# A message-passing layer on one core: the edge loop in pairs of tiles, with semaphores and one-hot buffers per target tile

## The reference, cut to what matters

```
msgs = x[src]; s = segment_sum(msgs, dst); c = segment_sum(1, dst)
agg  = s / maximum(c, 1)
x    = x + (agg @ W_l.T + x_norm @ W_r.T + b_r)     # x_norm: the rows of x, normalised
... layer norm and RMS norm of the new rows, attention over the 625 rows with rotary embedding
```

## Time and profile before

| what | value |
|---|---|
| median of three runs | 1066.08 us |
| profiled execution, its span | 1070.24 us, 1068.4 us |
| PE busy | 967.0 us (91%) |
| DVE, ACT, POOL busy | 466.6, 278.7, 130.2 us |
| edge matmuls (line 568) | 480 records, 55.0 us busy |
| granted PE clock over the span | 0.942 |

### The profile page before, as it was taken

One profiled execution on the slowest core, in us unless ns is written; L12 is line 12 of the kernel. 1 busy time (PEld: TensorE's weight loads), 2 busy tenths in 40 slices (PEclk: granted clock), 3 DMA queues, 4 the chain that ended last, 5 costly groups with the idle time before them and its releaser, 6 DMA issues.

```text
span 1068.4 us, 15246 instructions
## 1 busy us (share of the span) xinstructions
PE 967.0 (91%) x5585; PEld 782.8 (73%) x5585; DVE 466.6 (44%) x1426; ACT 278.7 (26%) x624; POOL 130.2 (12%) x135
## 2 busy tenths in 40 slices
PE   5999899889999999889998989999999998899896
PEld 5988454789999867688976768777786554566785
DVE  6658634542222330452259997522435143332222
ACT  3110034212222012313336764232111111124010
POOL 3010000023231110024410000000101000000241
PEclk9899778999999989999988999899899999899998
DMA  9100000138897512229542000053200000231762
GB/s 330 67 0 1 1 1 0 49 114 331 308 334 279 187 65 80 69 86 306 175 143 83 1 2 1 30 195 139 79 1 1 1 1 1 118 118 53 245 227 73
DMA packets 26278, 114.71 MB, mean 107 GB/s; under 512 B 5096, under 2 KB 9102, under 8 KB 19050
## 3 DMA queue, kind: packets, MB, share of 16 engines
q1 hardware_dynamic: 20647, 97.09, 25.5%
q0 software_dynamic: 5568, 16.78, 4.8%
HBM read 102.05 MB, written 11.81 MB: 107 GB/s over the span
## 4 chain that ended last, share of the span: by engine, by line
PE 71%; DVE 13%; DMA 6%; issue 5%; ACT 3%; POOL 1%; SPq 1%; DVEq 0%; POOLq 0%; ACTq 0%
PE PS L726 7%; PE PS L415 6%; PE PS L568 5%; PE PS L784 4%; PE PS L741 4%; PE PS L1110 4%; PE PS L770 3%; PE PS L392 3%; PE PS L426 3%; PE PS L484 3%; DMA arena<-flat_rows,route 3%; PE PS L806 2%; DVE arena L1806 2%; PE PS L610 2%; PE PS L854 2%
## 5 line engine op out<-in xcount | busy, mean ns | idle before, releaser
L392 PE MATMUL PS<-const 128*128 128x128 f32 x780 | 103.9, 296 | 7.8 <-DVE X L1177 2.1
L392 PEld LDWEIGHTS PS<-const 128*128 128x128 f32 x780 | 99.4, 209 | 12.9 <-issue 4.2
L726 PEld LDWEIGHTS PS<-HT,ring 128*128 128x128 f32 x680 | 78.4, 192 | 3.4 <-issue 2.6
L726 PE MATMUL PS<-HT,ring 128*128 128x128 f32 x680 | 78.8, 275 | 2.2 <-DVE HT L1701 1.3
L2417 POOL DMA_INDIRECT slot_rows<-ST,route x46 | 46.4, 1009 | 169.1 <-ACT ST L2167 99.7
L2365 POOL TENSOR_TENSOR col<-col,power 125x5 f32<-125x5 f32 x8 | 9.4, 1177 | 454.9 <-DVE col L1192 344.8
L1698 DVE TENSOR_TENSOR HT<-HT,PS 128x256 f32<-128x256 f32 (+1 forms) x51 | 19.2, 376 | 93.6 <-ACT HT L2156 73.7
L568 PE MATMUL PS<-HT 125*125 125x250 bf16 x480 | 55.0, 277 | 3.4 <-DVE HT L1574 3.4
L568 PEld LDWEIGHTS PS<-HT 125*125 125x125 bf16 x480 | 53.5, 141 | 3.8 <-DVE HT L1574 3.8
L928 PE MATMUL PS<-arena,HT 125*33 125x125 f32 x400 | 53.7, 283 | 0.0
L741 PE MATMUL PS<-ring,HT 128*128 128x256 f32 x204 | 46.7, 379 | 0.0
(11 more groups left out here) (430 smaller groups left out, 1736.0 us busy)
## 6 DMA issues: line engine op xcount, KB each, us to landing
ring<-in_experts SPq DMA_DIRECT2D x17, 1386.0 KB
ring<-in_experts SPq DMA_DIRECT2D x17, 768.0 KB, 5.8
ring<-in_experts SPq DMA_DIRECT2D x11, 1026.0 KB
arena<-in_experts SPq DMA_DIRECT2D x6, 1026.0 KB
ring<-in_experts SPq DMA_DIRECT2D x6, 1024.0 KB, 7.9
arena<-in_experts SPq DMA_DIRECT2D x6, 1024.0 KB
arena<-in_gnn SPq DMA_DIRECT2D x5, 1024.0 KB, 5.8
ring<-in_experts SPq DMA_DIRECT2D x8, 513.0 KB, 3.7
```

What stands on the lines that cost most here:

```text
L392: pe.matmul(PS[:, bank, 0:128], ident, ident, start=True, stop=True)
L726: mm = pe.matmul(PS[:, bank, at:at + SLOTS], both[:, j, k, m * 128:(m + 1) * 128], xs[0][i % 2][:, k, :], start=(k == 0), stop=(k == KD - 1))
```

## The change

- `GE` is 2: the runs are found in pairs of edge tiles. Each d always does the two tiles of its first pair outside the loop, and the loop does four tiles a turn. From the same targets this gives 18, 22, 18, 18 and 18 edge tiles, 94 in all.
- Each d has its own `onehots` and `edge_mm` semaphore, and even and odd d have one-hot buffers of their own, four tiles each. `shifts` and the third register load are gone: PE loads one register for each d (`further`), DVE two (one for d = 0).
- The count comes from two matmuls of 200 columns in place of one of 400, and DVE's reduction of line 1505 is gone; the 24 filler matmuls behind the count become 20. ACT makes the casts of the two number patterns, which DVE made.
- Two W_r products and the sum of tile 0 move from behind d = 2 to behind d = 1; the sum of tile 1 is alone behind d = 2 with three W_r products; behind d = 3 and d = 4 PE's work is as before. On DVE `both_types` and `finish` come ahead of the register loads of the next d, and the tiles 1 and 2 are finished later or one step apart.
- POOL's addition of the bias row waits for the sixth ACT copy, that is, until after the loop of d = 1.
- The causal mask is filled ahead of the last `finish`; POOL takes the two powers in two instructions of five columns; XN is written behind the copies of the transposes (`residual_norm`).

```diff
-GE = 4
+GE = 2
...
-        onehots, edge_mm = sem("onehots"), sem("edge_mm")
+        onehots, edge_mm = ([sem(f"{x}{d}") for d in range(NT)] for x in ("onehots", "edge_mm"))
...
+        src_hot = [HT[0:TP, r * hot_size:r * hot_size + 4 * 313].bitcast(BF16).rearrange("p (q n) -> p q n", q=4)
+                   for r in range(2)]
+        dst_hot = [HT[0:TP, r * hot_size + 4 * 313:(r + 1) * hot_size].bitcast(BF16).rearrange("p (q n) -> p q n", q=4)
+                   for r in range(2)]
...
-                mm = pe.matmul(PS[0:1, 7, 0:NT * ET], above[:, 0, 0:1], inside_flat, start=True, stop=True)
+                pairs = inside_flat.rearrange("p (g q) -> p g q", q=GE)
+                for q in range(GE):
+                    mm = pe.matmul(PS[0:1, 7, 0:NT * NG], above[:, 0, 0:1], pairs[:, :, q], start=(q == 0), stop=(q == GE - 1))
...
-                for _ in range(24):
+                for _ in range(20):
...
-                    if d == 2:
-                        for t in range(NT):
-                            root_tile(side_bank(), XT, wr_, t * TP, TP).then_inc(act_full, 1)
-                    for t in {2: (0, 1), 3: (2,), 4: (3,)}.get(d, ()):
-                        sum_tile(t, side_bank()).then_inc(act_full, 1)
+                    for t in {1: (0, 1), 2: (2, 3, 4)}.get(d, ()):
+                        root_tile(side_bank(), XT, wr_, t * TP, TP).then_inc(act_full, 1)
+                    if d:
+                        sum_tile(d - 1, side_bank()).then_inc(act_full, 1)
...
-                def limits(d):
-
-                    if d == 1:
-                        pe.wait_ge(ranges_ready, 2)
-                    start = pe.value_load(ranges[0:1, d:d + 1], min_val=0, max_val=NG - 1)
-                    stop = pe.value_load(ranges[0:1, NT + d:NT + d + 1], min_val=1, max_val=NG)
-                    return start, stop, pe.value_load(ranges[0:1, 2 * NT + d:2 * NT + d + 1], min_val=0, max_val=NT * NG)
+                def further(d):
+
+                    return pe.value_load(ranges[0:1, d:d + 1], min_val=0, max_val=NG - 1)
...
-                    with pe.Fori(start, stop) as i:
-                        for q in range(GE):
-                            pe.wait_ge(onehots, shift * GE + i * GE + (q + 1))
-                            for m in range(NT):
-                                mm = pe.matmul(PS[0:TP, base + m // 2, m % 2 * 2 * TP:(m % 2 + 1) * 2 * TP],
-                                               src_hot[:, q, m * TP:(m + 1) * TP], dst_hot[:, q, :],
-                                               start=False, stop=False)
-                            mm.then_inc(edge_mm, 1)
+                    for q in range(2):
+                        pe.wait_ge(onehots[d], q + 1)
+                        edge_tile(q)
+                    with pe.Fori(0, more, 2) as i:
+                        for q in range(4):
+                            pe.wait_ge(onehots[d], 2 * i + (q + 3))
+                            edge_tile((q + 2) % 4)
...
+            def residual_norm():
+
+                mv = col[:, 64:64 + NT * 2].rearrange("p (t s) -> p t s", t=NT)
+                dve.wait_ge(rms_ready, 1)
                 for t in range(NT):
                     ins = dve.tensor_scalar(XN[:, t, :], X[:, t, :], mv[:, t, 0:1], col[:, 8 + t:9 + t],
                                             ALU.subtract, ALU.mult)
...
-                dve.wait_ge(patterns_out, 2)
-                dve.tensor_copy(iota16, numbers[:, 0:626]).then_inc(patterns_ready, 1)
-                dve.tensor_copy(target16.rearrange("p d c -> p (d c)"), numbers[:, 626:626 + 2 * NT * TP]
-                                ).then_inc(patterns_ready, 1)
...
-                dve.tensor_reduce(found, PS[0:1, 7, 0:NT * ET].rearrange("p (d g q) -> p d g q", d=NT, q=GE), AX.X,
-                                  ALU.add).then_inc(dve_free, 7)
-                dve.wait_ge(dve_free, 7)
...
-                def shifts():
-
-                    link(dve.tensor_tensor(lim[:, 3, :], lim[:, 1, :], lim[:, 0, :], ALU.subtract))
-                    link(dve.memset(lim[:, 2, :], float(NG)))
-                    for d in range(1, NT):
-                        link(dve.tensor_tensor(lim[:, 2, d:d + 1], lim[:, 2, d - 1:d], lim[:, 3, d - 1:d], ALU.add))
-                    link(dve.tensor_tensor(lim[:, 2, :], lim[:, 2, :], lim[:, 0, :], ALU.subtract))
-                    dve.tensor_copy(ranges[:, 2 * NT + 1:3 * NT], lim[:, 2, 1:NT]).then_inc(ranges_ready, 1)
+                def further(d):
+
+                    first = dve.value_load(ranges[0:1, NT + d:NT + d + 1], min_val=0, max_val=NG) if d else 0
+                    return first, dve.value_load(ranges[0:1, d:d + 1], min_val=0, max_val=NG - 1)
...
-                    dve.wait_ge(act_free, 15 + t)
+                    dve.wait_ge(act_free, (12, 16, 17, 18)[t])
...
-                    with dve.Fori(start, stop) as i:
-                        for q in range(GE):
-                            j = bass.ds(i * GE + q, 1)
-                            dve.wait_ge(edge_mm, shift * GE + i * GE + (q + 1))
-                            dve.tensor_scalar(src_hot[:, q, :], iota16, srcf[:, j], None, ALU.is_equal)
-                            dve.tensor_scalar(dst_hot[:, q, :], target16[:, d, :], keyf[:, j], None,
-                                              ALU.is_equal).then_inc(onehots, 1)
-                    if d == 0:
-                        shifts()
-                    if d + 1 < NT:
-                        start, stop, shift = limits(d + 1)
+
+                    def edge_tile(q, j):
+
+                        dve.tensor_scalar(src_hot[d % 2][:, q, :], iota16, srcf[:, j], None, ALU.is_equal)
+                        dve.tensor_scalar(dst_hot[d % 2][:, q, :], target16[:, d, :], keyf[:, j], None,
+                                          ALU.is_equal).then_inc(onehots[d], 1)
+
+                    for q in range(2):
+                        edge_tile(q, bass.ds(first * 2 + q, 1))
+                    with dve.Fori(0, more, 2) as i:
+                        for q in range(4):
+                            dve.wait_ge(edge_mm[d], 2 * i + (q + 3))
+                            edge_tile((q + 2) % 4, bass.ds((first + i) * 2 + (q + 2), 1))
                     if d:
                         both_types(d - 1)
-                    for t in {3: (0,), 4: (1, 2)}.get(d, ()):
-                        finish_taken(t)
+                    if d in (2, 3):
+                        finish_taken(d - 2)
+                    if d + 1 < NT:
+                        first, more = further(d + 1)
...
+                finish_taken(NT - 3)
                 finish_taken(NT - 2)
+                dve.memset(ahead_mask[:, 0:N - TP], 0.0)
+                dve.wait_ge(tables_in, 32)
+                dve.tensor_copy(ahead_mask[:, N - TP:N], CONST(const, "causal", TP))
...
                 layer_and_rms_norm()
                 take_transposes(XT, scale=COLS(cols, "ln1_w"))
+                residual_norm()
...
+                act.wait_ge(patterns_out, 1)
+                act.activation(iota16, numbers[:, 0:626], ACT.Copy).then_inc(patterns_ready, 1)
+                act.wait_ge(patterns_out, 2)
+                act.activation(target16.rearrange("p d c -> p (d c)"), numbers[:, 626:626 + 2 * NT * TP], ACT.Copy
+                               ).then_inc(patterns_ready, 1)
...
             pool.wait_ge(xn_ready, NT)
+            pool.wait_ge(act_free, 6)
             pool.tensor_tensor(X[:, :, :], X[:, :, :], ROWS(rows, "l0_b_r", TP).unsqueeze(1).broadcast_to([TP, NT, D]),
                                ALU.add).then_inc(root_added, 1)
             pool.wait_ge(root_added, 1)
             for t in range(NT):
-                pool.wait_ge(act_free, 10 + t)
+                pool.wait_ge(act_free, 10 + t + (t > 1))
                 pool.tensor_tensor(X[:, t, :], X[:, t, :], ROOT[:, t, :], ALU.add).then_inc(root_added, 1)
             pool.wait_ge(var_ready, 2)
-            two = col[:, 0:208].rearrange("p (a n) -> p a n", a=2)
-            pool.tensor_tensor(two[:, :, 8:8 + NT], two[:, :, 0:NT], power[:, :].unsqueeze(1).broadcast_to([TP, 2, NT]),
-                               ALU.pow).then_inc(rstd_ready, 1)
+            pool.tensor_tensor(col[:, 112:112 + NT], col[:, 104:104 + NT], power[:, :], ALU.pow).then_inc(rstd_ready, 1)
+            pool.tensor_tensor(col[:, 8:8 + NT], col[:, 0:NT], power[:, :], ALU.pow).then_inc(rms_ready, 1)
```

82 lines of the change are left out of this document (41 added, 41 removed).

## The result

| | before | after |
|---|---|---|
| median, first chip | 1068.19 us (1058.96 to 1071.42, 4 runs) | 1049.11 us (1044.76 to 1053.44, 4 runs) |
| median, second chip | 1066.04 us (1060.91 to 1069.42, 11 runs) | 1047.56 us (1043.15 to 1050.09, 6 runs) |
| profiled execution, its span | 1070.24, 1068.4 us | 1044.76, 1042.8 us |
| granted PE clock over the span | 0.942 | 0.958 |
| first score matmul of the attention | 127.83 us | 111.29 us |

The ratio is 0.9841 [0.9802, 0.9880] on the first chip and 0.9814 [0.9787, 0.9841] on the second: 17 and 20 us less (the brackets hold a 95% interval; the difference of the first chip's medians, taken by itself, is 19 us). The forecast was 1052 us, in 1044 to 1062.

A forecast was written before the change was run, and what follows sets the result against it. PE was taken as the bound, through its gaps and slow clock in the first 125 us. Terms summed to 12.15 us, 17.65 with the clock: 1053.9 or 1048.4 from the 1066.08 median, 1052.6 from the profile; forecast 1052, range 1044 to 1062.

The forecast's parts named there:

- Term 1: Start, ahead of the first edge matmul: fewer register loads and an earlier edge key save 2.1 us (ends 1.3 and 2.5).
- Term 2: Loop of d = 0: moving POOL's bias row addition beside PE's W products saves 2.2 us (ends 2.2 and 0).
- Term 3: Ahead of PE's transposes: without the shifts most of the 2.25 us wait goes, saving 1.5 us (ends 1.0 and 2.0).
- Term 4: Edge loops: 94 tiles for 96, at 0.545 us a tile, save 1.1 us.
- The rival that DVE becomes the pace: Edge loops: DVE's tile time over 0.545 us costs 0.9 us per 0.01 over 94 tiles; at 0.65, 1062 us; chance 0.04.
- Terms 5 to 7: PE's waits between loops shrink: loads at d = 1 and 2 save 1.0 us, d = 3 0.65, d = 4 1.2.
- Term 8: Loop of d = 1: with both long gaps ahead gone, the clock recovers, saving 2.5 us, transposes included (ends 0 and 2.7).
- Term 9: Norm behind the last sum: earlier mask, five-column powers and XT copies not behind XN save 2.4 us (end 1.4).
- Term 10: Projection to rotary part: with shorter gaps PE runs at 2.4 GHz, 11.5 us for 14.5, saving 3.0 (ends 0 and 3.0).
- the stall moved: First rival: POOL's additions meet DVE's tiles for d = 2 or d = 3, giving 1056 us; chance 0.12.
- the clock fell again: Rival: transposes alone or half-microsecond gaps bring the clock down, leaving a gain of 8 to 10 us, 1057; chance 0.12.
- the attention did not get slower: Rival, slower: attention starts in another phase and half of a possible clock loss gives 1078 us; chance 0.06.

The follow-up runs named there:

- Three loads: The changed kernel with three register loads for each target tile on both engines, as before, the further values unused; 1050.43 us (1 run).
- Casts on DVE: The changed kernel with the two pattern casts back on DVE, ahead of the copy of dst; 1043.42 us (1 run).
- shifts back: The changed kernel with the chain of the shifts back on DVE behind the loop of d = 0, results unused; 1046.79 us (4 runs), ratio 0.9828.
- bias row early: The changed kernel with POOL's addition of the bias row early again, waiting only for the normalised rows; 1043.38 us (1 run).
- XT first: Two versions of the changed kernel: ACT copies the transposes ahead of the adjacency, 1045.86 us (6 runs); the same with six filler matmuls added, 1043.79 us (6 runs).
- loads first: The changed kernel with DVE's register loads ahead of `both_types` and the finish, and one finish moved; 1049.20 us (1 run).
- norm order back: The changed kernel with the mask, the power of ten columns and XN where before has them; 1047.46 us (4 runs), ratio 0.9829.
- side work back: The changed kernel with W_r products and sums where before has them, and tile 1's finish behind the last addition of types; 1038.12 us (1 run).

## Why the prediction was right

The forecast, 1052 us, is 3 us above the first chip's median and 4 above the second's. It was right by its terms of order, which the runs bear out; that the sum came so near is in part luck, as the terms show. From the two profiles, each term with what it measured:

- **Term 1, start, 2.1 forecast:** 2.0, of which 0.33 is the key (done at 8.17, forecast 8.1) and 1.68 the gap. Three loads gives the loads 1.24 of the gap. The other 0.44 (2.64 before, 2.20 there) goes with the two tiles outside the loop; no run has that alone. Casts on DVE shows no more than 0.2.
- **Term 2, POOL's stand, 2.2:** 2.2, shown from both sides.
- **Term 3, shifts, 1.5:** the 2.25 us wait is gone and 0.2 of it came back as a longer way through the transposes, so 2.0. Up to 0.6 of this is clock: the transposes took 2.37 us in before and 1.73 in after, waits left out. By order it is 1.4. The size is near, but the chain alone was not the cause: the wait was the chain and three loads in a row (shifts back), and with one load left the chain costs nothing.
- **Term 4, tiles, 1.1:** 1.3. The five loops at full clock are 4 x 9.84 + 11.98 = 51.3 us against 8.98 + 13.05 + 8.77 + 2 x 10.91 = 52.6 before. The rival that DVE becomes the pace is out: a tile takes 0.547 us.
- **Terms 5 to 7, between loops, 1.0 + 0.65 + 1.2:** 1.5 + 0.9 + 1.2. I took a third of each wait to stay with one load of three; nothing stayed. One load leaves no idle time on PE at all.
- **Term 8, clock in the loop of d = 1, 2.5:** 0.7. This step failed. With the transposes, which it included at 0.3, it is at most 1.3. Both long gaps are gone, and after's profile still has 0.60 from 22 to 26 us. Before's loop in its own timeline:

```profile
28.23 15.40 PE L568 MATMUL PS<-HT 125*125 125x250 bf16 x120
```

The forecast had the slow clock there as the work of the two gaps; the runs show it without them and, in bias row early, a gap without it. In the profiles of the changed code the slow stretch, about 1.5 us, lies in the loop of d = 1 twice, in that of d = 0 four times (XT first twice, loads first, three loads), and nowhere five times. After, norm order back and side work back have the same order of work until the loop of d = 1 ends; the first lost it, the other two didn't. So it is not set by the order alone. The three profiles of before's code all have it (2.6, 1.9 and 1.3 us; with the new norm order it lies in the last 15 matmuls of d = 0). Two of them, with PE standing 2.25 and 1.85 us ahead of the transposes, have 0.50 for over six us (27 to 33, 23 to 29); in the other twelve profiles no such stretch in these loops lasts over four us. That the change makes it rarer or shorter is possible by this; it is not shown. The Trainium skill ("TensorE: Matmul & The Clock Gate", What's actually happening) says that the number of slow matmuls differs from run to run; these rows agree, and I should have given term 8 a smaller share.
- **Together, to the last sum, 12.25:** 12.13. The rows above add up to 11.8, and 0.3 lie in the joins between them. That it comes so near is luck: the order gave more (terms 4 to 6) and the clock less, by about as much.
- **Term 9, norm, 2.4:** 2.3. Side work back shows that 1.2 us of it hang on where the finish of tile 1 stands, which I had at nothing. POOL's power of five columns took 1.20 us, not 1.44.
- **Term 10, clock in the projection, 3.0:** 2.4. From the projection's start to the end of the rotary part it is 12.07 us (94.93 to 107.00) for 14.48. The mechanism held and the size was off: the first tile takes 2.09 us, not 1.7, and DVE's tiles follow each other at 2.02, not 1.95. (I had read 11.2 us for the whole projection; it is 11.63, the row being cut at 120 us.) This clock, unlike that of term 8, goes with the order: 3 of 3 slow and 11 of 11 fast.

Between the rotary part and the first score matmul 0.3 us is lost. To the first score matmul this gives 16.5 us of 17.65. The median time fell by 19 (12.8 to 21.1 by the interval of the ratio), which 16.5 fits. The two spans differ by 25.6, so 9.1 us lie behind 111 us, where no instruction was changed. From the first score matmul to the end the three profiles of before's code take 936.7 to 940.6 us and the eleven of after's 926.4 to 937.2. The means are 939.0 and 932.6, so some 6 us of gain beyond the forecast may lie there. Some of the 9.1 is the attention (to the first matmul of the next part 96.7 us in before's profile, 92.4 in both others of its code, 92.3 after). The remainder is open; no experiment went there. Against the profiled execution's 1070.24, from which the sum was taken, the forecast of 17.65 is 8 us short of the 25.5 that the profiled execution of after shows.

Of the rivals, the stall moved only to where it costs nothing (POOL's additions of ROOT at 57.16 lengthen three one-hots, 1.4 us in all, and PE does not wait; those at 42.66 meet no DVE work), the clock fell again in one of two places, DVE did not become the pace, and the attention did not get slower.

The Trainium skill's rule on the port pair ("SBUF — State Buffer", Who interferes with whom), named with the first rival, agrees with the bias row early: 2.90 us for a one-hot of 0.28. By the rule POOL and a DVE instruction that takes the shared pair cannot run side by side, so it matters what DVE does meanwhile. At 39.20 it does not work; at 57.16 it does, and the rows agree again (0.88 us for 0.39).

## What to carry to other kernels

A clock that falls behind two gaps in every profile, and recovers when the gaps are shortened, can be counted on; one that falls in a long, evenly busy stretch may be the luck of one profile, so look at more than one execution before pricing it. A wait can be two things in a row: here a serial chain and the register loads that had to come behind it. Take each away alone before you price it; the terms of one stretch need not add up. Count the register loads on a queue that others wait for, and start with the work that lies ahead of a serial tail (here one finish, 1.2 us), even if nothing waits for it where it stands.
